# A graph network and a selected LSTM on one core: TensorE's last 12 scatter rounds written as a loop

## What is computed

```
# 1. graph part: 1250 nodes x 512, 21250 weighted edges (src, dst)
xn    = rows of layernorm(x), scaled to length 1
sup   = edge_weight * exp(sim / (2 sigma_sq))   # sim: product of the two rows' xn, 0 on the diagonal
norm  = segment_sum(sup, src)
10 times: out = (x*b + (segment_sum(sup * out[dst], src) + out) * a) / (b + norm*a + a)
x = x + out
# 2. LSTM over the 1250 rows, one after the other, with 4 sets of weights
for each row x_t:
    s = argmax([h, c, x_t] @ W_sel.T + b_sel)            # which of the 4 sets
    g = x_t @ W_ih[s].T + h @ W_hh[s].T + b_ih[s] + b_hh[s]
    h, c = lstm(g, c)
x = x + all h
```

## Time and profile before

| | us |
|---|---|
| runs before: median (lowest to highest) | 6814.86 (6814.09 to 6822.49) |
| the profiled execution, its own time | 6817.24 |
| its span, first to last instruction | 6815.5 |
| mean granted TensorE clock in it | 0.959 of full speed |

### The profile page before, as it was taken

One profiled execution on the slowest core, in us unless ns is written; L12 is line 12 of the kernel. 1 busy time (PEld: TensorE's weight loads), 2 busy tenths in 40 slices (PEclk: granted clock), 3 DMA queues, 4 the chain that ended last, 5 costly groups with the idle time before them and its releaser, 6 DMA issues.

```text
span 6815.5 us, 340711 instructions
## 1 busy us (share of the span) xinstructions
PE 6117.3 (90%) x126674; PEld 4119.5 (60%) x126675; DVE 3616.7 (53%) x19152; ACT 1805.4 (26%) x6561; POOL 1686.4 (25%) x4128
## 2 busy tenths in 40 slices
PE   6727999789999999999999999999999999999986
PEld 3523444666666666666666666666666666666663
DVE  5553111245565556555665555566556655556555
ACT  1001000522332223223332333233333333233321
POOL 4733111412222222222222222222222222222220
PEclk8758999589999999999999999999999999999999
DMA  3230000622222122122222222222222222222210
GB/s 95 1 77 0 0 0 0 192 71 58 62 63 58 57 60 65 55 60 60 65 63 60 62 61 60 60 63 63 61 60 65 64 61 63 59 63 62 61 52 27
DMA packets 691011, 389.94 MB, mean 57 GB/s; under 512 B 47835, under 2 KB 670811, under 8 KB 690720
## 3 DMA queue, kind: packets, MB, share of 16 engines
q1 hardware_dynamic: 659746, 369.66, 18.5%
q0 software_dynamic: 24192, 0.10, 1.1%
q10 hardware_dynamic: 7038, 19.69, 0.9%
HBM read 370.96 MB, written 18.38 MB: 57 GB/s over the span
## 4 chain that ended last, share of the span: by engine, by line
PE 70%; DVE 6%; issue 5%; DMA 1%; DVEq 0%; SPq 0%; ACT 0%; POOL 0%; POOLq 0%
PE ps L1016 33%; PE ps L1078 15%; PE ps L1025 8%; PE ps L1009 5%; PE ps L1005 4%; DVE hsum L843 2%; PE ps L1002 2%; PE ps L991 1%; DVE osum L851 1%; DVE acts L861 1%; DVE gates L848 1%; DVE osum L854 1%; DMA wring<-in_w_ih 1%; DVE cprod L857 0%; PE ps L978 0%
## 5 line engine op out<-in xcount | busy, mean ns | idle before, releaser
L1016 PE MATMUL ps<-WH,hparts 128*2 128x384 f16 x49760 | 2303.0, 326 | 196.6 <-issue 176.1
L1016 PEld LDWEIGHTS ps<-WH,hparts 128*2 128x2 f16 x49760 | 1053.4, 83 | 1044.7 <-issue 292.9
L843 DVE TRANSPOSE_TENSOR_REDUCE hsum<-ps 128x12 f32<-128x384 f32 x1250 | 728.7, 583 | 1793.0 <-PE ps L1016 1788.0
L1078 PE MATMUL ps<-xcur,wcur 128*128 128x64 f32 x9728 | 1341.9, 281 | 85.7 <-issue 12.4
L1078 PEld LDWEIGHTS ps<-xcur,wcur 128*128 128x128 f32 x9728 | 1178.5, 191 | 273.3 <-issue 210.2
L454 POOL COPY xT<-hfull 128x4 f32 x1250 | 239.5, 192 | 3727.2 <-DVE hfull L872 3727.2
L470 POOL COPY wcur<-wring 128x512 f32<-128x512 f32 x1216 | 743.4, 611 | 445.1 <-ACT gxb L598 443.3
L1025 PEld LDWEIGHTS ps<-WH,hparts 128*2 128x2 f16 x40000 | 603.7, 83 | 352.7 <-issue 314.9
L1025 PE MATMUL ps<-WH,hparts 128*2 128x128 f16 x40000 | 781.2, 219 | 7.5
L583 ACT ACTIVATE gx_now<-gxb 128x16 f32 x1250 | 269.7, 216 | 1782.2 <-DVE pick L837 1707.1
L969 PE MATMUL ps<-O,Adj 128*128 128x512 f16 x3000 | 650.3, 380 | 77.2 <-DVEq L748 77.2
(11 more groups left out here) (147 smaller groups left out, 4983.8 us busy)
## 6 DMA issues: line engine op xcount, KB each, us to landing
wring<-in_w_ih SPq DMA_DIRECT2D x1280, 256.0 KB, 2.9
gxb<-in_w_hh ACTq DMA_DIRECT2D x32, 512.0 KB, 5.6
adjacency<-Adj SPq DMA_DIRECT2D x2, 6400.5 KB, 24.7
Adj<-adjacency SPq DMA_DIRECT2D x10, 640.0 KB, 7.5
sim<-adjacency SPq DMA_DIRECT2D x10, 640.0 KB, 6.3
adjacency<-total,where_ POOLq DMA_INDIRECT x168
x_rows<-X SPq DMA_DIRECT2D x1, 2560.0 KB, 8.7
wring<-x_rows SPq DMA_DIRECT2D x10, 256.0 KB, 3.5
```

The source lines that it names most:

```text
L843: dve.tensor_reduce(hsum[:, :], gate_ps.rearrange("p (c q) -> p c q", q=32), AX.X, ALU.add, apply_transpose=True).then_inc(turned, 1)
L1016: last = nc.tensor.matmul(gate_ps[32 * j:32 * j + 2, :], hparts[:, k, :], WH[:, s * KC + k, part, j, 0:3 * P], start=(k == 0 and part == 0 ...
L1078: last = nc.tensor.matmul(unit_ps, wcur[:, k, :], xcur[:, k, :], start=(k == 0), stop=(k == KC - 1))
```

## The change

TensorE's rounds 30 to 41 are no longer written out. A loop of the engine runs their body 12 times; its waits compare with a register, and the column of `ew` is addressed by a register.

```
-            for i in range(EIT):
+            for i in range(RT * NCH):
                 for b in range(NQ):
                     pe.wait_ge(kd_ready[b], i + 1)
                     nc.tensor.matmul(key_ps[b], ones[:, :], kdiag[:, b, :], start=True, stop=True).then_inc(kr_ready[b], 1)
...
-                if i < RT * NCH:
-                    similarity(i // NCH, i % NCH)
+                similarity(i // NCH, i % NCH)
+            with pe.Fori(RT * NCH, EIT) as i:
+                n = pe.snap(i + 1)
+                for b in range(NQ):
+                    pe.wait_ge(kd_ready[b], n)
+                    nc.tensor.matmul(key_ps[b], ones[:, :], kdiag[:, b, :], start=True, stop=True).then_inc(kr_ready[b], 1)
+                for b in range(NQ):
+                    pe.wait_ge(same_ready[b], n)
+                    nc.tensor.matmul(total_ps[b], same[:, b, :], ew[:, bass.ds(i * NQ + b, 1)],
+                                     start=True, stop=True).then_inc(total_mm[b], 1)
```

## The result

| | us |
|---|---|
| before, 8 runs: median (lowest to highest) | 6817.83 (6814.09 to 6823.33) |
| after, 8 runs | 6797.75 (6794.53 to 6800.25) |
| ratio after / before, 95% interval | 0.9969 (0.9959 to 0.9979) |
| profiled execution after: span, granted clock | 6798.5, 0.959 |

The changed kernel is 20 us faster, 0.31%. That is more than the 0.2% that the measurement can tell, and outside the range forecast. The granted clock is the same (0.959 in both profiles), so the time does not come from a faster TensorE.

A forecast was written before the change was run, and what follows sets the result against it. GpSimd was taken to pace the scatter rounds and TensorE's LSTM steps to end last. Pauses removed (-22.1), set 0's new pause (+22.5) and start-up (+1) summed to +1.4 us: 6816.3 us on the median, range 6802 to 6833.

The forecast's parts named there:

- The loop itself: TensorE's scatter rounds: loop instructions cost 0, hidden in the wait for `kdiag`; upper bound 1 us, or 4 without that cover.
- Only the loop counts: Rival: pauses merely move among themselves or aren't tied to code-block edges; 6814.9 us, chance 0.12.
- The places: LSTM steps: code behind the rounds moves 344 instructions ahead, so each 256-instruction block edge stands 88 instructions later.
- L1057 of set 2: Edge just ahead of this register operation in `guessed`: forecast 0; as slower rival, 42 us more, 6858 us, chance 0.07.
- instruction 19 of set 3: New edge in L1005 of `guessed` set 3: cost 0, its copy being reached 0.17 us before `tanc`.
- (b): `repeated` set 1, first loop: pause behind the first weight load goes, 0.17 us in 61 steps, -10.4 us.
- (c): `repeated` set 3, first loop: pause behind the fourth instruction goes, median 1.18 to 1.08 us, 70 steps, -7.0 us.
- (a): `guessed` set 2, weight loads of L1005: pause behind the 14th instruction goes, -4.7 us.
- set 0's pause: `guessed` set 0, L1005: new edge behind instruction 11 makes `pick` 0.12 us later in TensorE-bound steps, +22.5 us; bounds +17.6, +38.
- start-up term: First passes through the steps' code: set 0's copy spans two blocks, other stalls as before; +1 us, at most +3.
- Set 0's pause is covered: Faster rival: the new pause in `guessed` set 0 is hidden and the gains stay; 6794 us, chance 0.10.
- The two slower ones: Rivals: a pause at L1057, 6858 us, chance 0.07; set 0 paying the whole pause, 6832 us, chance 0.08.

The follow-up runs named there:

- after + 344: Changed kernel plus 344 idle semaphore instructions on TensorE behind the scatter rounds, putting later code back where it stood before: 6810.9 us, ratio 1.0000.

## Why the prediction was wrong

By means of the four profiles of each kernel, after less before, in us:

| part | forecast | measured |
|---|---|---|
| ahead of the first step (the loop in it) | 0 | -2.1, mostly chance |
| first 19 steps | +1 | -6.1 |
| first loop: steps repeated with sets 1 and 3 | -17.4 | -16.3 |
| steps guessed as set 2, rightly | -4.7 with the repeated ones | -2.3 |
| steps guessed as set 0, rightly | +22.5 with the repeated ones | +6.1 |
| all other steps | 0 | +0.2 |
| second loop | 0 | +3.5 |
| behind the last step | 0 | -0.6 |
| sum | +1.4 | -17.6 |

The runs give -20.1, with an interval from -14 to -28 (0.9959 and 0.9979 of 6817.8).

- **The loop itself: right.** It costs 0 and gains 0, and the cover named for it (the wait for `kdiag`) is where it lies. "Only the loop counts" is refuted as a rival by the kernel before with 168 idle instructions.
- **The places: right.** The block of 256 instructions, the three pauses that go, and the one that comes in L1005 of set 0, ahead of its fourth load, are in the profile as forecast. So are the edges without a price, L1057 of set 2 and instruction 19 of set 3: set 3's steps differ by 0.0 us.
- **Terms (b) and (c): right.** All repeated steps of the first loop together (-16.3 with sets 1 and 3, +0.2 with sets 0 and 2) are -16.1. They hold a share of the other two terms, since each such step began with a guess. 77 of them guess set 0, where `pick` is 0.035 us later in the mean (+2.7 us), and 85 guess set 2, where it is 0.022 earlier (-1.9). Without these shares the pauses that went are -16.9 us, against -17.4.
- **Term (a): right.** -2.3 and -1.9 are -4.2, against -4.7.
- **The size of set 0's pause is the step that failed.** The prediction let the pause end 0.31 us behind the copy's register operation, had `pick` 0.12 us later in each step that TensorE bounds, and so came to +22.5 us. The place was right, and so was the number of steps; the size was wrong.
  - *The steps.* I count as bound by TensorE those steps guessed as set 0 in which the first load of L1009 starts more than 0.2 us behind the end of `tanc` in the first profile of before: 185, and 185 times 0.12 is 22.2.
  - *The size.* In the same 185 steps, the first profile of after against the first of before, the fourth load of L1005 starts 0.25 us behind the register operation in the median (0.20 before), and the last load of the logits is 0.05 us later in the mean (0.03 in the median). `pick` follows these loads one for one: it is 0.05 us later in the mean, and the two delays agree step by step (correlation 0.94). The other three profiles of after give the same means. That makes 185 times 0.05, 9 us, and the table has 6.1 in the 236 rightly guessed steps and 2.7 in the repeated ones.
  - *The bound.* The lower bound of 17.6 fell too. It took set 2's pause, 0.095 us, as the least, and only 37% of the 185 steps have a delay of 0.08 us or more. So L1005's loads of set 0 are 0.29 us in the median and not above 0.33, as the forecast of the profile had them; step 689, shown above with 0.36, is among the long ones. Why the same edge delays by nothing in one step and by 0.10 us in another stays open.
  - *The other outcome.* The kernel with 8 idle instructions shows how near it was: with the edge 8 instructions earlier the last load and `pick` are 0.13 us later in the mean, and the rightly guessed steps cost +19.3.
- **The start-up term failed too, in its sign.** I looked only at set 0's copy, which spans two blocks now, and said "other stalls as before". They weren't. Most of the gain, 4.8 of the 6.1 us in the mean, lies in one step, the third, which is the first that is repeated, and with set 1: from the 2nd to the 3rd `hsum` after is 4.3 to 5.4 us shorter in all four pairs of profiles. Before, the edge behind the first load of `repeated` set 1 is crossed there for the first time, with a stop of 3.50 us, and a branch of L1038 behind it takes 0.86 us. After has neither. The loads of that step in the timelines, second profile of before and then of after:

```profile
1405.06 0.08 PEld L1016 LDWEIGHTS ps<-WH,hparts 128*2 128x2 f16 x1 [1.16 <-issue]
1408.64 0.32 PEld L1016 LDWEIGHTS ps<-WH,hparts 128*2 128x2 f16 x11 [3.50 <-issue]
```
```profile
1399.48 1.08 PEld L1024 LDWEIGHTS ps<-WH,hparts 128*2 128x2 f16 x32 [0.93 <-issue]
```

The queue of code fetches shows three fetches in this step before (1404 to 1416 us) and none after (1396 to 1410 us). In the whole execution there are 22 fetches after, against 26 in the earlier trace rows:

```profile
q8 instruction: 22, 0.36, 0.0%
```

Stalls ahead of the first `hsum` changed as well, but brought nothing. The branches of L1032 and L1038 stall 3.7 us each in the second profile of before, those lines after (L1040, L1046) 3.3 between them; sequencer rows, ns, before and then after:

```profile
L1038 PEldq COMPARE_BRANCH  x805: 65/202/3733, 1384.2 to 6772.1; - x161
```
```profile
L1032 PEldq COMPARE_BRANCH  x1555: 67/77/3746, 1380.4 to 6779.7; - x195
```
```profile
L1046 PEldq COMPARE_BRANCH  x805: 65/202/221, 1380.5 to 6753.7; - x161
```
```profile
L1040 PEldq COMPARE_BRANCH  x1555: 67/87/3326, 1377.1 to 6761.4; - x195
```

Yet from the start of that first branch to the first `hsum` it is 9.3 to 11.2 us in the four profiles of before and 10.4 to 11.9 after.

- **The second loop was left out.** Its 34 steps have edges of their own (6 instructions into `repeated` for set 0, 9 for set 2) and a first pass. There the jump behind the first step's output products (L1061 before, L1069 after) stalls 3.3 to 3.8 us instead of 1.8, and that is half of the +3.5. The six steps repeated with set 0, whose loads take 1.34 us in the median instead of 1.07, cost 1.5 us more.
- **The rivals.** "Set 0's pause is covered", at 6794 us, comes nearest, with 0.10. It was right about the direction and wrong about the size of the pause. That its sum is so near is in part luck: set 0's 9 us and the second loop's 3.5 were made up for by the 8 us ahead of the 20th step, which it did not have either. The two slower ones fell: nothing shows at L1057, and the whole pause is paid only with the edge at instruction 3. The chance of 0.63 for a cancellation of -22 against +22.5 was too much for a sum of two terms of which one had bounds of 17.6 to 38 from one nearest row.

The rule weighed in the prediction, from the Trainium skill, Runtime: NRT & Kernel Launch, section Instruction fetch mechanics, says that crossing a block edge is mostly hidden. Here it is for most edges and not for all: in the median 0.17 to 0.18 us show in `repeated` behind instruction 1, 3 or 6 of a set to which `of_set` takes a branch (0.11 behind 4 of set 3, to which it takes none), and in the mean 0.04 to 0.13 us in `guessed` of set 0. The measurement decides. The same section's warning, that a taken branch to code not held forces a fetch before the engine goes on, agrees with the stalls of 3.3 to 5.1 us at branches in the first passes.

## What to carry to other kernels

In a loop with branches that runs a thousand times, where an edge between blocks of 256 instructions falls just behind a taken branch, and nothing is queued on the engine, each crossing cost 0.04 to 0.18 us here. A change of code far ahead of the loop moves these edges, so its effect must be told from its own work: put idle instructions in the place of those removed, and see whether the gain stays. A few idle instructions can be worth more than the change, and should be set last, since any later edit moves the edges again.

## What was not expected of the hardware

- Moving code by 8 idle instructions alone changed the time by 0.3% (0.9969 for after, 1.0001 with 8 more).
- The pause is reproducible to 0.01 us from one kernel to another in the same step (1.24, 1.15 and 1.21 us in before and in after + 344), though from step to step it varies between nothing and 0.27 us (loads of 1.08 to 1.35 us in the steps repeated with set 1).
- Code in a body of five blocks is not fetched again, 22 fetches in all with 1216 passes, and crossing an edge still pauses.
- The first crossing is of another size: the edge that later costs 0.17 us a pass stopped TensorE for 3.50 us when it was first reached.
- The shorter the way from the last taken branch to the edge, the longer the delay of the logits' last load in `guessed` of set 0: means of 0.13, 0.05 and 0.04 us over the 185 steps, with the edge behind instructions 3, 11 and 19.
